# Attention 1 of a four-layer kernel: the sums over heads on GpSimd, two heads at a time, instead of strided sums on VectorE

## The chip, the cores and the metric

The kernel runs on one core of a Trainium2 chip. The time is device time in microseconds, the median of the timed runs. A core has five engines with a queue of their own each: TensorE (PE, with its weight loads shown as PEld), VectorE (DVE), ScalarE (ACT), GpSimd (POOL) and SyncE (SP), which here issues most DMAs. Engines wait for each other by semaphores that are written out by hand.

## The reference

Eight sequences of 256 tokens of width 256 go through four layers; each adds a cross attention over `ctx_1024` and then a feed-forward network. The change touches the attention of layer 1, whose softmax runs over the heads, not over the keys:

```python
    def _L1_xattn_ref(query, key, value, Wq_w, Wq_b, Wk_w, Wk_b, Wv_w, Wv_b, Wo_w, Wo_b):
        ...
        scale = 1.0 / jnp.sqrt(jnp.float32(HEAD_DIM))
        energy = jnp.einsum('bhqd,bhkd->bhqk', Qh, Kh) * scale
        attn = jax.nn.softmax(energy, axis=1)
        out = jnp.einsum('bhqk,bhkd->bhqd', attn, Vh)
        out = out.transpose(0, 2, 1, 3).reshape(b, -1, D_MODEL)
        return out @ Wo_w.T + Wo_b
```

With 16 heads of width 16, 256 queries and 256 keys, each (key, query) pair needs the maximum and the sum of 16 numbers, one for each head.

## The kernel before

The program goes through eight stages one after the other: attention 0, ffn 0, attention 1, ffn 1, and so on. Attention 1 lies from about 599 to 990 us of the profiled execution. It works in eight slots, one for each batch element `b`, and each slot handles two halves `t` of the keys (128 keys on the partitions; a row of `probs[:, t]` holds 16 heads x 256 queries in f32, 4096 elements).

In slot `b` (function `slot1` on each engine) the order is this:

- TensorE computes the scores once for the maxima (`for_maxima`, L871), two heads to a PSUM bank, first for `t` = 0, then for `t` = 1. Between them stand the products of the probabilities of the slot before with its values (`values1`, L808), which wait for the semaphore `norm1`.
- ScalarE copies the first two banks of each half to `M2` (L1361), VectorE takes the running maximum (L1802), folds it (L1804, L1806) and splits it in two bf16 parts (L1808, L1810).
- TensorE computes the scores a second time less the maxima (`less_maxima`, L885 and L888), ScalarE takes the exponentials two heads at a time (`exps1`, L1352, eight for each `t`, sixteen in a row), and each adds one to `exp1_done`.
- VectorE adds a bias to the values of the next element (`take_values`, L1722 and L1734) and then runs `sums1(b, 0)` and `sums1(b, 1)`. Each forms the sum over heads, its reciprocal (L1828) and the product of the 4096 probabilities with it (L1830, `norm1`). For `t` = 0 the sum is two reductions of eight heads (L1821) and an add (L1823), for `t` = 1 one reduction of sixteen (L1826); all read `probs` as "p h q -> p q h", so that neighbours in the reduction lie 256 elements apart. `rest_k` (L1697, `kr` <- `kf`, `KP`) stands between the two calls.
- After that VectorE still has `rest_q` (L1702), the residual (L1789), the statistics (L1606) and the low parts of keys and queries (L1706, L1710) before the maxima of the next slot.

GpSimd's part of attention 1 is one instruction ahead of the slots, `X` <- `X` + `bog` (L583, 128x4096 f32 with two inputs from SBUF). VectorE waits for it before slot 0. After it GpSimd has nothing until ffn 1. The routing stage of ffn 3 also has two adds of this kind on GpSimd (L630, 128x1280 bf16).

Of the kernel before, what the change touches and what calls it, by code (L numbers as in the profile page):

```python
# [12 lines left out]
ALU = mybir.AluOpType  # L13
ACT = mybir.ActivationFunctionType
AX = mybir.AxisListType
# [5 lines left out]
B, S = 8, 256  # L21
T = B * S
NT = T // P
ST = S // P
H, DH = 16, 16
HALF = 2
HPH = H // HALF
# [20 lines left out]
DIGIT_BITS, DIGITS, UNROLL0 = 2, 15, 3  # L48
# [25 lines left out]
def program(nc, a, out, stages):  # L74
    ctx = ExitStack()
    with ctx:
        def sem(name):
            return ctx.enter_context(nc.semaphore(name))

        def sb(name, shape, dt, c=ctx):  # L80
            return c.enter_context(nc.sbuf_tensor(name, shape, dt))
# [71 lines left out]
        probs = sb("probs", [P, ST, H, S], F32, att)  # L153
# [3 lines left out]
        hpart = sb("hpart", [P, 2, S], F32, att)  # L157
        hsum = sb("hsum", [P, ST, S], F32, att)
# [126 lines left out]
                 "xnt_psum xnt_done w_loaded qk_loaded bias_ready bias_added ctx0 ctx1 q_psum k_psum v_psum q_evac k_evac q_r1 "  # L285
                 "k_r1 q_mid k_mid q_split k_split pack0 pack1 pack_k0 pack_k1 padrow0 padrow1 v_copied v_ready smax_ps smax_done mT_ps m_hi m_lo mrow0 "
                 "mrow1 st_ps exp_done av_done o_out oT_ps on_rden on_norm o2_ps on_ready y_ps x_res mask_loaded mask_ready pad_out "
                 "nmax_ready rsum_ready vs_ready p1_ps p1_max m1_step m1_ready p2_ps exp1_done sum1_step norm1 av1_done x_ffn stored "
                 "pack_const pack_rows rt_const rt_logits rt_step rt_exp rt_cnt rt_prefix thr_step thr_cmp thr_cnt "
                 "xn_out0 xn_out1 xn_out2 xn_out3 rows_ready "  # L290
                 "experts_w0 experts_w1 experts_w2 experts_w3 experts_w4 experts_w5 experts_w6 experts_w7 "
# [4 lines left out]
                 "f3_router f3_place f3_gates f3_loaded f3_hot f3_list f3_idx "  # L296
                 "gather0 gather1 gather2 gather3 f3_xt f3_xgT f3_up f3_w1_act f3_w1_dve f3_mid f3_down f3_yg f3_scatter").split()
        s = {n: sem(n) for n in names}
        ctx_sem = [s["ctx0"], s["ctx1"]]
        pack = [s["pack0"], s["pack1"]]  # L300
        pack_k = [s["pack_k0"], s["pack_k1"]]
# [20 lines left out]
        def pack_keys(eng, par, done):  # L322
            for j, part in enumerate(K_PARTS):
                eng.dma_start(Kpack[par][DH * j:DH * (j + 1)].rearrange("d (e f) t -> d e (f t)", f=HALF),  # L324
                              KP[par][:, part]).then_inc(done, 16)
# [13 lines left out]
        def ready_x(eng, n):  # L339

            if n == 0:
                for half in range(2):
                    eng.wait_ge(s[f"x_load{half}"], 16)
                return
            kind, L = stages[n - 1]
            if kind == "att":
                eng.wait_ge(s["x_res"], FREE + 8 * (order["att", L] + 1))
            else:
                eng.wait_ge(s["x_ffn"], 1 + sum(k != "att" for k, _ in stages[:n - 1]))
# [194 lines left out]
        def _(pool):  # L544
# [26 lines left out]
            def attention(n, L):  # L571
                i = order["att", L]
                if n > 0:
                    ready_x(pool, n)
                if L in SOFTMAX_KEYS:
                    pool.wait_ge(s["k_split"], 8 * i + 1)
                    pool.wait_ge(s["pack_rows"], 64 * (m_order[L] + 1))
                    pack_keys(pool, 0, pack_k[0])

                if L != 0:  # L580
                    pool.wait_ge(s["bias_ready"], 2 * i + 2)
                    pool.wait_ge(s["xn_ready"], 8 * (ln_order["att", L] + 1))
                    pool.tensor_tensor(X[:], X[:], bog[:].unsqueeze(1).to_broadcast([P, NT, D]), ALU.add)\  # L583
                        .then_inc(s["bias_added"], 1)
                if L in SOFTMAX_KEYS:

                    for b in range(1, B):


                        pool.wait_ge(s["m_lo"], 8 * m_order[L] + b)  # L590
                        pack_keys(pool, b % 2, pack_k[b % 2])

            def rows_sent(n):

                pool.wait_ge(s["rows_ready"], 6 * 16 * (g_order[stages[n]] + 1))
                for j in range(LNB):
                    pool.wait_ge(xn_out[j], SENT0 + 16 * (PAIRS // LNB) * (g_order[stages[n]] + 1))
# [48 lines left out]
            for n, (kind, L) in enumerate(stages):  # L646
                if kind == "att":
                    attention(n, L)
                elif L in (0, 3):
                    (ffn0 if L == 0 else ffn3)(n)  # L650
                elif L == 1:
                    pool.wait_ge(s["f1_rmax"], 1)
                    pool.partition_all_reduce(rall[:], rmax[:], P, bass.bass_isa.ReduceOp.max).then_inc(s["f1_rall"], 1)
# [903 lines left out]
        def _(dve):  # L1557
# [105 lines left out]
            def attention(n, L):  # L1663
# [147 lines left out]

                def sums1(b, t):

                    steps = 4 if t == 0 else 2
                    base = 6 * b + 4 * t
                    if t == 0:

                        for half in range(2):
                            hh = slice(half * HPH, (half + 1) * HPH)
                            dve.wait_ge(s["exp1_done"], 16 * b + 4 * (half + 1))  # L1820
                            dve.tensor_reduce(hpart[:, half], probs[:, t, hh].rearrange("p h q -> p q h"), AX.X, ALU.add).then_inc(s["sum1_step"], 1)  # L1821
                        dve.wait_ge(s["sum1_step"], base + 2)
                        dve.tensor_tensor(hsum[:, t], hpart[:, 0], hpart[:, 1], ALU.add).then_inc(s["sum1_step"], 1)  # L1823
                    else:
                        dve.wait_ge(s["exp1_done"], 16 * (b + 1))
                        dve.tensor_reduce(hsum[:, t], probs[:, t].rearrange("p h q -> p q h"), AX.X, ALU.add).then_inc(s["sum1_step"], 1)  # L1826
                    dve.wait_ge(s["sum1_step"], base + steps - 1)
                    dve.reciprocal(hsum[:, t], hsum[:, t]).then_inc(s["sum1_step"], 1)  # L1828
                    dve.wait_ge(s["sum1_step"], base + steps)
                    dve.tensor_tensor(probs[:, t], probs[:, t], hsum[:, t].unsqueeze(1).to_broadcast([P, H, S]), ALU.mult)\  # L1830
                        .then_inc(s["norm1"], 1)

# [39 lines left out]
                def slot1(b, par, v):  # L1872
                    nearer, later = exists(b + 1), exists(b + 2)
                    maxima1(b, 0)
                    maxima1(b, 1)
                    if nearer:
                        take_values(b + 1, 1 - par)
                    sums1(b, 0)
                    if later:
                        rest_k(b + 2, par)  # L1880
                    sums1(b, 1)
                    if later:
                        rest_q(b + 2, par)
                    if exists(b - 1):
                        residual(b - 1)
                    if later:
                        low_k(b + 2, par)
                        low_q(b + 2, par)
# [285 lines left out]
            def route3(n):  # L2174
# [25 lines left out]
                for j in range(2):  # L2200
                    e = dve.tensor_tensor(row_m[:, j], row_m[:, 3 + j], row_m[:, 5], ALU.mult)
                chain(e)
                running_counts(2 * E3, lambda _, e: chain(e), 0, r)
                for j in range(PAIRS3):
                    of = slice(j * E3, (j + 1) * E3)
# [173 lines left out]
```

## Time and profile before

| | us |
|---|---|
| median of 3 runs | 2509.2 |
| lowest | 2507.66 |
| highest | 3518.86 |
| span of the profiled execution | 2506.0 |

Two of the three runs lie within 1.6 us of each other, the third stands alone. The profiled execution's span is 3.2 us below the median; those lie around the span. Engine busy times in the span: PE 2005.9 us, DVE 1279.5, ACT 810.5, POOL 242.8. Busy share is an average over eight stages with different limits. Attention 1 has its own: in the 401 us from 599 to 1000, DVE is busy for 356.28 us, PE for 261.48, ACT for 135.01 and POOL for 10.00, with a mean granted clock of TensorE of 0.80.

### The profile page before, as it was taken

To read this page: it belongs to the slowest core of one execution; us is meant where nothing else is said; L and a number is where in the kernel's file an instruction comes from. 1 tells how busy PE (TensorE), PEld (TensorE's weight loads), DVE (VectorE), ACT (ScalarE), POOL (GpSimd) and SP (SyncE) were. 2 spreads that over 40 slices of the span, in tenths; PEclk is the share of its full clock that TensorE was granted. 3 is DMA by queue.
4 is the path that set the end of the run, shared out by engine and by line. 5 is a ranking of instruction groups with operands and counts; after the bars stand their busy time and mean duration, and the time that the engine had idled before them with its cause. 6 is when DMAs were issued, how large, how long until landed. Compare 5 with 4: busy or idle time off the path is not lost.

```text
span 2506.0 us, 33028 instructions
## 1 busy us (share of the span) xinstructions
PE 2005.9 (80%) x11527; PEld 1280.2 (51%) x11528; DVE 1279.5 (51%) x2283; ACT 810.5 (32%) x1752; POOL 242.8 (10%) x234
## 2 busy tenths in 40 slices
PE   5999983594767755478998999999996676399998
PEld 3556543473534533334444444444444444389997
DVE  5334325516998997844442545453536666522221
ACT  3343331122433422334443521111115765122221
POOL 1010100341000000020110000000001000023333
PEclk9999995796878877579999999999998987599999
DMA  4342305126224210144431400000005541642222
GB/s 109 46 57 32 52 8 215 26 36 130 33 30 54 30 26 5 40 52 59 60 40 13 186 1 1 1 1 1 1 1 93 80 63 26 239 131 38 35 36 30
DMA packets 91386, 132.86 MB, mean 53 GB/s; under 512 B 13428, under 2 KB 80508, under 8 KB 88060
## 3 DMA queue, kind: packets, MB, share of 16 engines
q1 hardware_dynamic: 75900, 103.84, 19.7%
q0 software_dynamic: 15360, 27.28, 6.9%
q8 instruction: 86, 1.41, 0.3%
q14 instruction: 40, 0.33, 0.0%
HBM read 64.09 MB, written 16.26 MB: 32 GB/s over the span
## 4 chain that ended last, share of the span: by engine, by line
PE 59%; DVE 19%; DMA 8%; issue 6%; ACT 4%; SPq 4%; DVEq 0%; POOL 0%; POOLq 0%; ACTq 0%
PE ps L1137 13%; PE ps L808 10%; PE ps L1215 6%; PE ps L1226 5%; DMA Qpack<-QP 3%; PE ps L852 3%; PE ps L771 3%; PE ps L799 2%; DVE hpart L1821 2%; DVE hsum L1826 2%; DMA Kpack<-pad_rows 2%; SPq L446 2%; PE ps L1047 2%; PE ps L1037 2%; PE ps L1111 2%
## 5 line engine op out<-in xcount | busy, mean ns | idle before, releaser
L808 PE MATMUL ps<-pT,V 128*32 128x256 f32 x1536 | 298.5, 408 | 40.3 <-DVE V L1759 40.3
L1740 DVE TENSOR_REDUCE mx<-ps 128x2 f32<-128x512 f32 x256 | 165.6, 686 | 169.4 <-PE ps L774 92.5
L1337 ACT ACTIVATE pT<-ps 128x512 f32<-128x512 f32 x256 | 150.5, 597 | 243.2 <-PE ps L802 140.7
L799 PE MATMUL ps<-Qpack,Kpack 99*128 99x256 bf16 (+1 forms) x768 | 168.2, 289 | 40.5 <-ACT pT L1342 16.6
L808 PEld LDWEIGHTS ps<-pT,V 128*32 128x32 f32 x1536 | 104.7, 112 | 163.2 <-issue 63.3
L1215 PEld LDWEIGHTS ps<-xgT,XNT 128*128 128x128 f32 x1280 | 151.4, 194 | 2.0
L1215 PE MATMUL ps<-xgT,XNT 128*128 128x128 f32 x1280 | 151.5, 277 | 0.0
L1226 PE MATMUL ps<-w,mid 128*128 x640 | 144.6, 379 | 0.0
L771 PE MATMUL ps<-Kpack,Qpack 97*128 97x256 bf16 x512 | 107.9, 287 | 40.8 <-DMA Kpack<-pad_rows 22.7
L1342 ACT ACTIVATE pT<-ps,nmax 128x256 f32<-128x256 f32 x256 | 118.0, 496 | 56.5 <-DVE nmax L1750 55.7
L799 PEld LDWEIGHTS ps<-Qpack,Kpack 99*128 99x128 bf16 (+1 forms) x768 | 70.3, 102 | 123.1 <-ACT pT L1337 42.9
L808 PE MATMUL ps<-probs,V 128*32 128x256 f32 x512 | 66.5, 526 | 83.0 <-DVE probs L1830 83.0
L1226 PEld LDWEIGHTS ps<-w,mid 128*128 128x128 f32 x640 | 118.6, 190 | 14.5
L1137 PE MATMUL ps<-partA,h 128*128 128x512 bf16 x512 | 116.4, 379 | 0.2
L1137 PE MATMUL ps<-partB,h 128*128 128x512 bf16 x512 | 115.7, 379 | 0.0
L1750 DVE TENSOR_REDUCE nmax<-ps 128x2 f32<-128x512 f32 x128 | 84.6, 688 | 52.3 <-PE ps L799 51.8
L1533 ACT ACTIVATE mid<-ps 128x512 f32<-128x512 f32 x80 | 43.4, 595 | 208.2 <-PE ps L1215 202.9
L324 POOL DMA_DIRECT2D Kpack<-KP x96 | 51.2, 540 | 538.9 <-DVE MR L1745 453.7
L674 PE MATMUL ps<-ident,xn 128*128 128x128 f32 x224 | 43.8, 364 | 73.7 <-DVE xn L1656 64.5
L771 PEld LDWEIGHTS ps<-Kpack,Qpack 97*128 97x128 bf16 x512 | 44.8, 99 | 101.9 <-DVE mx L1740 41.3
L2113 DVE TENSOR_TENSOR xn<-hA 128x512 f32<-128x512 f32 x64 | 44.3, 692 | 102.8 <-ACT hA L1508 100.3
L583 POOL TENSOR_TENSOR X<-X,bog 128x4096 f32<-128x4096 f32 x3 | 26.4, 8814 | 627.2 <-DVE bog L1691 620.4
(312 smaller groups left out, 3733.0 us busy)
## 6 DMA issues: line engine op xcount, KB each, us to landing
Qpack<-QP SPq DMA_DIRECT2D x192, 128.0 KB, 6.9
w<-in_w SPq DMA_DIRECT2D x19, 1024.0 KB, 6.8
Kpack<-KP POOLq DMA_DIRECT2D x96, 128.0 KB, 5.6
Kpack<-KP SPq DMA_DIRECT2D x96, 128.0 KB, 4.2
ctxT<-in_ctxT SPq DMA_DIRECT2D x32, 256.0 KB, 5.9
h<-in_h SPq DMA_DIRECT2D x2, 4096.0 KB, 22.2
wd<-in_wd SPq DMA_DIRECT2D x4, 1536.0 KB, 14.9
xn_rows<-xn SPq DMA_DIRECT2D x16, 256.0 KB, 2.8
```

Source lines behind the costliest of these rows:

```text
L324: eng.dma_start(Kpack[par][DH * j:DH * (j + 1)].rearrange("d (e f) t -> d e (f t)", f=HALF), KP[par][:, part]).then_inc(done, 16)
L771: mm = pe.matmul(A[2 + h % 2][:, t], Qpack[par][0:MASK_ROW + 1, h, t * P:(t + 1) * P], Kpack[par][0:MASK_ROW + 1, h], start=True, stop=L != 0)
L799: mm = pe.matmul(A[h % ring][:, t], Kpack[par][0:rows, h, t * P:(t + 1) * P], Qpack[par][0:rows, h], start=True, stop=L != 0)
L808: mm = pe.matmul(O[c // 2][r0:r0 + VW, c % 2], V[par][:, t, h], weights[:, t], start=t == 0, stop=t == ST - 1)
L852: mm = pe.matmul(P1[:, t], lhs[:, c, t * P:(t + 1) * P], wo[:, c], start=c == 0, stop=c == tiles - 1)
L1137: mm = pe.matmul(bank, high(w_), part[:, v - 1, c] if v else high(src[:, c]), start=v + c == 0, stop=v == 2 and c == HT - 1)
L1215: mm = pe.matmul(bank[:, f % 4 * P:(f % 4 + 1) * P], w1_tile[k % 2][:, c, f * P:(f + 1) * P], xgT3[k % 2][:, c], start=c == 0, stop=c == K ...
L1226: mm = pe.matmul(ps[5 + 2 * (k % 2)][:, 0], mid3[k % 2][:, c], w2_3[:, ds(e, 1), c].squeeze(1), start=c == 0, stop=c == HT - 1)
L1337: act.activation(pT[h % 4][:], A[h % 2][:], ACT.Exp).then_inc(s["exp_done"], 1)
L1342: e = act.activation(pT[h % 8][:, t], A[h % 4][:, t], ACT.Exp, bias=nmax[:, t, h:h + 1], accum_out=esum[:, t, h:h + 1])
L1740: dve.tensor_reduce(mx[:, :, h], A[2 + h % 2][:], AX.X, ALU.max).then_inc(s["smax_done"], 1)
L1750: dve.tensor_reduce(nmax[:, :, h], A[h % 4][:], AX.X, ALU.max, negate=True).then_inc(s["nmax_ready"], 1)
```

## The change

In `sums1` on VectorE the three reductions and the add go. It now waits for `sum1_done`, then takes the reciprocal and multiplies as before. The new function `head_sums` on GpSimd makes the sum: for each `b` and `t` one add of two pairs of heads into `hpart` (128x512), six more adds of a pair each onto `hpart`, and one add of its two halves into `hsum[:, t]` (128x256). The seven adds wait for the exponentials pair by pair, and each waits for the add before it by `sum1_part`, a new name for the semaphore `thr_cnt`, which ffn 0 has left at 15 (`DIGITS`). The first add of a call waits for the end of the call before, the last add for `norm1` of the same half of the slot before. All sixteen calls follow on GpSimd's queue behind the add of L583.

```diff
...
-                 ... exp1_done sum1_step norm1 av1_done x_ffn stored "
+                 ... exp1_done sum1_done sum1_step norm1 av1_done x_ffn stored "
...
+        s["sum1_part"] = s["thr_cnt"]
...
@@ -582,6 +584,10 @@
                     pool.wait_ge(s["xn_ready"], 8 * (ln_order["att", L] + 1))
                     pool.tensor_tensor(X[:], X[:], bog[:].unsqueeze(1).to_broadcast([P, NT, D]), ALU.add)\
                         .then_inc(s["bias_added"], 1)
+                if L == 1:
+                    for b in range(B):
+                        for t in range(ST):
+                            head_sums(b, t)
                 if L in SOFTMAX_KEYS:
 
                     for b in range(1, B):
@@ -589,6 +595,22 @@
 
                         pool.wait_ge(s["m_lo"], 8 * m_order[L] + b)
                         pack_keys(pool, b % 2, pack_k[b % 2])
+
+            def head_sums(b, t):
+
+                k = DIGITS + 7 * (ST * b + t)
+                pool.wait_ge(s["exp1_done"], 16 * b + 8 * t + 2)
+                if b + t:
+                    pool.wait_ge(s["sum1_done"], ST * b + t)
+                pool.tensor_tensor(hpart[:], probs[:, t, 0:2], probs[:, t, 2:4], ALU.add).then_inc(s["sum1_part"], 1)
+                for e in range(2, H // 2):
+                    pool.wait_ge(s["exp1_done"], 16 * b + 8 * t + e + 1)
+                    pool.wait_ge(s["sum1_part"], k + e - 1)
+                    pool.tensor_tensor(hpart[:], hpart[:], probs[:, t, 2 * e:2 * e + 2], ALU.add).then_inc(s["sum1_part"], 1)
+                pool.wait_ge(s["sum1_part"], k + 7)
+                if b:
+                    pool.wait_ge(s["norm1"], ST * (b - 1) + t + 1)
+                pool.tensor_tensor(hsum[:, t], hpart[:, 0], hpart[:, 1], ALU.add).then_inc(s["sum1_done"], 1)
 
             def rows_sent(n):
 
@@ -1811,22 +1833,9 @@
 
                 def sums1(b, t):
 
-                    steps = 4 if t == 0 else 2
-                    base = 6 * b + 4 * t
-                    if t == 0:
-
-                        for half in range(2):
-                            hh = slice(half * HPH, (half + 1) * HPH)
-                            dve.wait_ge(s["exp1_done"], 16 * b + 4 * (half + 1))
-                            dve.tensor_reduce(hpart[:, half], probs[:, t, hh].rearrange("p h q -> p q h"), AX.X, ALU.add).then_inc(s["sum1_step"], 1)
-                        dve.wait_ge(s["sum1_step"], base + 2)
-                        dve.tensor_tensor(hsum[:, t], hpart[:, 0], hpart[:, 1], ALU.add).then_inc(s["sum1_step"], 1)
-                    else:
-                        dve.wait_ge(s["exp1_done"], 16 * (b + 1))
-                        dve.tensor_reduce(hsum[:, t], probs[:, t].rearrange("p h q -> p q h"), AX.X, ALU.add).then_inc(s["sum1_step"], 1)
-                    dve.wait_ge(s["sum1_step"], base + steps - 1)
+                    dve.wait_ge(s["sum1_done"], 2 * b + t + 1)
                     dve.reciprocal(hsum[:, t], hsum[:, t]).then_inc(s["sum1_step"], 1)
-                    dve.wait_ge(s["sum1_step"], base + steps)
+                    dve.wait_ge(s["sum1_step"], 2 * b + t + 1)
                     dve.tensor_tensor(probs[:, t], probs[:, t], hsum[:, t].unsqueeze(1).to_broadcast([P, H, S]), ALU.mult)\
                         .then_inc(s["norm1"], 1)
```

## Rows read from the trace of the kernel before

**Rows 1.** The page: span, and busy time of each engine.
```profile
span 2506.0 us, 33028 instructions
PE 2005.9 (80%) x11527; PEld 1280.2 (51%) x11528; DVE 1279.5 (51%) x2283; ACT 810.5 (32%) x1752; POOL 242.8 (10%) x234
```

**Rows 2.** Waits, 599 to 1000 us: waiter <- releaser: total us, times, longest.
```profile
PE ps L808 <- DVE probs L1830: 83.0, 8, 16.5
```

**Rows 3.** Chain that ended last, 765 to 815 us: start us, us, what.
```profile
769.01 7.34 DVE hpart L1821 x2
...
783.64 7.03 DVE hsum L1826
```

**Rows 4.** Timeline of DVE, 757 to 860 us: start us, us, engine, line, operation.
```profile
768.05 0.49 DVE L1734 COPY V<-Vb 128x256 f32<-128x256 f32 x2
769.01 7.33 DVE L1821 TENSOR_REDUCE hpart<-probs 128x256 f32<-128x2048 f32 x2 [0.46 <-ACT probs L1352]
776.37 0.43 DVE L1823 TENSOR_TENSOR hsum<-hpart 128x256 f32<-128x256 f32 x1
776.83 1.75 DVE L1828 RECIPROCAL hsum<-hsum 128x256 f32<-128x256 f32 x1
778.61 4.42 DVE L1830 TENSOR_TENSOR probs<-probs,hsum 128x4096 f32<-128x4096 f32 x1
782.96 0.68 DVE L1697 TENSOR_TENSOR kr<-kf,KP 128x512 f32<-128x512 f32 x1
783.56 7.10 DVE L1826 TENSOR_REDUCE hsum<-probs 128x256 f32<-128x4096 f32 x1
790.70 1.75 DVE L1828 RECIPROCAL hsum<-hsum 128x256 f32<-128x256 f32 x1
792.48 4.43 DVE L1830 TENSOR_TENSOR probs<-probs,hsum 128x4096 f32<-128x4096 f32 x1
```

**Rows 5.** ACT: one line's instructions (durations ns min/median/max), then its timeline.
```profile
L1352 ACT ACTIVATE probs<-ps x128: 597/597/599, 625.6 to 964.2; 128x512 f32<-128x512 f32 x128
...
766.38 10.60 ACT L1352 ACTIVATE probs<-ps 128x512 f32<-128x512 f32 x16 [2.70 <-PE ps L888]
...
814.07 10.55 ACT L1352 ACTIVATE probs<-ps 128x512 f32<-128x512 f32 x16 [2.70 <-PE ps L888]
```

**Rows 6.** POOL: one line's instructions, then its timeline in the first microseconds.
```profile
L583 POOL TENSOR_TENSOR X<-X,bog x3: 8799/8822/8822, 599.1 to 1902.6; 128x4096 f32<-128x4096 f32 x3
...
1.50 0.29 POOL L547 TENSOR_SCALAR_AFFINE_SELECT ident<-ident 128x128 f32<-128x128 f32 x1 [0.49 <-POOL ident L545]
...
2.42 0.19 POOL L555 MEMSET ones_bf<- 128x128 bf16 x1
2.69 0.29 POOL L557 TENSOR_SCALAR_AFFINE_SELECT upto<-upto 128x128 bf16<-128x128 bf16 x1
...
4.51 0.19 POOL L569 TENSOR_SCALAR spare<-row 128x1 f32<-128x1 f32 x1
```

**Rows 7.** POOL and DVE at the same time: timelines, and durations of single lines.
```profile
1902.63 8.82 POOL L583 TENSOR_TENSOR X<-X,bog 128x4096 f32<-128x4096 f32 x1 [591.15 <-DVE bog L1691]
1904.62 7.37 DVE L1697 TENSOR_TENSOR kr<-kf,KP 128x512 f32<-128x512 f32 x1 [1.54 <-ACT KP L1305]
...
L1734 DVE COPY V<-Vb x16: 278/290/8479, 599.5 to 911.5; 128x256 f32<-128x256 f32 x16
...
L630 POOL TENSOR_TENSOR lists<-lists,part x2: 2327/2950/3572, 2182.3 to 2184.5; 128x1280 bf16<-128x1280 bf16 x2
...
2182.28 3.66 DVE L2233 TENSOR_TENSOR lists<-lists,col 128x1280 bf16<-128x1280 bf16 x1 [0.15 <-DVE lists L2230]
...
2188.39 1.48 DVE L2235 TENSOR_TENSOR lists<-lists,part 128x1280 bf16<-128x1280 bf16 x1
```

**Rows 8.** Windows: engines' busy us (x count), granted clock, DMA share, GB/s.
```profile
788.00:797.00 9.00, 0.81 (x7) 0.25 (x8) 8.93 (x4) 0.42 (x1) 0.00 (x0) 0.55 0.00 0
801.00:805.00 4.00, 4.00 (x26) 1.54 (x28) 3.22 (x6) 0.00 (x0) 0.00 (x0) 0.50 0.84 143
```

More of the change, by code:

```diff
@@ L287, in program @@
                  "mrow1 st_ps exp_done av_done o_out oT_ps on_rden on_norm o2_ps on_ready y_ps x_res mask_loaded mask_ready pad_out "
-                 "nmax_ready rsum_ready vs_ready p1_ps p1_max m1_step m1_ready p2_ps exp1_done sum1_step norm1 av1_done x_ffn stored "
+                 "nmax_ready rsum_ready vs_ready p1_ps p1_max m1_step m1_ready p2_ps exp1_done sum1_done sum1_step norm1 av1_done x_ffn stored "
                  "pack_const pack_rows rt_const rt_logits rt_step rt_exp rt_cnt rt_prefix thr_step thr_cmp thr_cnt "
```

## The prediction, made before the changed kernel ran

> **What bounds the kernel now.** The page's engine totals [rows 1] say little here, since they mix eight stages, so I read attention 1 alone. The waits of its stretch come first [rows 2]: TensorE waits eight times, once a slot, for `probs` of L1830, 83.0 us in all, up to 16.5 us at a time. TensorE is not the limit of the slot's second half. The chain that ended last [rows 3] then shows who is: from the fourth exponential on it stays on VectorE, through the two reductions of L1821 and, after `kr`, the one of L1826. The timeline of VectorE [rows 4] gives one slot in full: 7.33 us for the two reductions, 0.43 for the add, 1.75 for the reciprocal, 4.42 for the product, `kr`, 7.10 for the third reduction, 1.75, 4.43, with no gap to speak of. The second product ends at 792.48 + 4.43 = 796.9 us, and TensorE's value products and VectorE's remaining duties both start from there. The exponentials are much shorter: the burst of sixteen begins at 766.38, the next slot's at 814.07 [rows 5], a period of 47.7 us, of which 796.9 - 766.4 = 30.5 us pass from the first exponential to the end of the second product. All that the change touches lies in these 30.5 us. The other 17 us start at the end of the second product and move with it.
>
> **What it removes.** Per slot, 7.33 + 0.43 + 7.10 = 14.9 us of VectorE, all on the chain: 8 x 14.9 = 119 us, if nothing took their place.
>
> **What it adds: the price of an add on GpSimd.** The trace has no f32 add of 128x512 there. The nearest row is L583, the same kind of add with 4096 elements, 8.82 us at most [rows 6]. In proportion, 512 elements take 8.82 / 8 = 1.10 us, and that is the lower bound, since it leaves out what an instruction costs whatever its size. An instruction on a single element a partition (L569) takes 0.19 us. With that as the fixed part, each element costs (8820 - 190) / 4095 = 2.11 ns, so 512 elements cost 0.19 + 1.08 = 1.27 us and 256 cost 0.73 us. I take these. (The Trainium skill, GPSIMD Engine Reference, section 3.1, gives 4497 ns for such an add of 2048 elements; a line through that figure and L583 would give 1.28 us for 512, so the sum would stay.) Each add also waits for the one before. The gap between dependent GpSimd instructions is 2.69 - (2.42 + 0.19) = 0.08 us between L555 and L557, and 0.49 us between L545 and L547 [rows 6]. I take 0.08, since L547 is the first of its kind in the program and may pay for that; 0.49 stays as the upper bound. One call is then 7 x (1.27 + 0.08) + 0.73 + 0.08 = 10.3 us, and two calls 20.5 us. At 1.10 us, 0.55 us and the same gap it is 8.9 us a call, and at a gap of 0.49 us it is 7 x 1.76 + 1.22 = 13.5 us. So GpSimd adds up more slowly than VectorE did (10.3 against 7.8 or 7.1 us), and any gain must come from lying beside other work.
>
> **What of it lies beside other work.** The exponentials are spaced (10.60 - 0.60) / 15 = 0.67 us, and the second one ends at 766.38 + 0.67 + 0.60 = 767.65 [rows 5]. GpSimd starts there, 1.36 us before VectorE could at 769.01. After that the exponentials come twice as fast as the adds, so it never waits for one again. While it makes the second sum, VectorE has the first reciprocal, the first product and `kr`: 1.75 + 4.42 + 0.68, 6.8 us that used to stand in the chain in full. This is where the change could win.
>
> **What takes it back.** The rows of both engines at the same time [rows 7] show that a GpSimd add and some VectorE instructions exclude each other for their whole length. While L583 ran from 1902.63 to 1911.45, VectorE's `kr` (two f32 inputs in SBUF, 0.69 us otherwise) took 7.37 us and ended at 1911.99. A copy `V` <- `Vb`, 0.29 us as a rule, took 8.48 us under another L583. It works in both directions: of the two L630 adds the first took 2.33 us and held up L2233 (3.66 us against 1.48 for L2235, the same shape), and the second, queued while L2233 finished, took 3.57 us. The product of L1830 has both inputs, `probs` and `hsum`, in SBUF, as `kr` has. I therefore count its 4.42 us and those of `kr` one after the other with GpSimd's adds, not beside them. (By the Trainium skill, SBUF — State Buffer, section "Who interferes with whom", a VectorE instruction with two SBUF inputs contends with a GpSimd instruction that reads SBUF, the second fully blocked, while one with a single input outside the 2-port modes does not contend. The trace agrees for `kr` and L2233. On the reciprocal the rule would leave the sum as it stands, and no row here shows it.) I let the reciprocal, with one input, run beside an add.
>
> **The sum for one slot**, on the clock of [rows 4]. GpSimd starts at 767.7. The two copies of L1734 (0.49 us, a form that was excluded in [rows 7]) get between its first adds: 0.5 us. First call 10.3 us: the first sum is ready at 778.5, where it was ready at 776.8 before. The reciprocal runs to 780.3 beside the first adds of the second call. The product waits for the add in progress, then holds GpSimd off for 4.4 us, and `kr` may follow at once, 0.6 us. The second call thus takes 10.3 + 4.4 + 0.6 = 15.3 us and ends at 793.8. Then reciprocal 1.75, product 4.43 and 0.1 us between instructions: 800.0, against 796.9. Each slot gets about 3 us longer. Which engine wins the port first hardly matters, because both sums, one product and `kr` must go through it in a row before the second reciprocal can start.
>
> Eight slots x 3.0 us = 24 us. The last slot has no `kr`, which changes it by 0.6. The profiled execution would take 2506.0 + 24 = 2530 us. The median of the runs shown lies 3.2 us above it, so 2533 us. TensorE's longer idle time costs nothing besides: its granted clock falls to the lower level of 1.2 GHz in this wait already (0.55 on the mean, 788 to 797 us) and is still there, at 0.50, from 801 to 805 us [rows 8], and those cold products are in the 17 us.
>
> The other pieces cost nothing. GpSimd's queue is empty in attention 1 but for L583, which ends before slot 0, and the change moves no DMA. The wait on `norm1` of the slot before has long been met. Behind VectorE's wait for the first sum stand `kr` and, from there on, the parts and residual of later elements. `kr` moves from 783.0 to 785.7 at the earliest, and its successors feed a slot that begins 28 us later. VectorE's idle 9 us or so while it waits gain nothing, since its order is fixed. If the cover of the first product is gone altogether, that is the sum above already.
>
> **Rivals.**
> 1. *No exclusion for L1830.* If the product runs beside the adds, the second sum is ready at 767.7 + 20.5 = 788.2 to 788.7, and the product ends 6.3 us later, at 794.5 to 795: 2 to 2.4 us a slot won, 16 to 19 us in all, about 2492. With adds of 1.10 us it is about 2470. For it: L1830 reads `hsum` as a broadcast, which no excluded row does. Against it: three instructions of [rows 7] were held up, with bf16 and f32 operands. It decides only if the product is exempt.
> 2. *Dearer adds.* The path has sixteen GpSimd instructions a slot, so each 0.1 us more on one of them costs 1.6 us a slot or 13 us in all. At the gap of 0.49 us each slot is 3.0 + 2 x 3.2 = 9.5 us longer, 2585 us. At 0.2 us more on each the change passes 2% (50 us). For it: two waits stand before each add where L557 had one. Against it: the gap between L555 and L557.
> 3. *Cheaper adds with exclusion*, 1.10 us: 3.0 - 2 x 1.4 = 0.2 us a slot, 2511 us. That is the break-even point of the forecast, and only an instruction with no fixed cost reaches it.
> 4. *The reciprocal excluded too.* Then up to 1.75 us a slot more, 2547 us.
>
> **How the numbers follow.** Exclusion and adds between the bounds, with cases 3 and 4 as its edges, 2505 to 2559 us: 0.73, best guess 2533. Dearer adds, beyond 2559 us: 0.15. No exclusion, below 2505 us: 0.12, of which 0.02 reaches 2459 us or less. The measurement can tell about 2% from no change, 50 us here, 2459 and 2559 us. So faster 0.02, same 0.83, slower 0.15. Range 2500 to 2563 us: below it lies most of the no-exclusion case (0.09), above it the rest of the dearer adds (0.11).
>
> **What would show each step.** Adds on GpSimd with a shortest duration of 1.27 us for 128x512 and 0.73 for 128x256; a pitch of 1.35 us in a row of them. In each slot one product of L1830 longer than 4.43 us, by what was left of the add in progress, and one GpSimd add of some 5 us that was held up behind it. `sum1_done` of the first half 12 us after the first exponential, the second product's end 33.6 us after it, a period of 50.7 us. VectorE idle some 9 us in the middle of a slot and again some 7 us after `kr`. A product of 4.42 us with GpSimd busy all through it would refute the exclusion; a pitch above 1.55 us would make the time pass 2%.

## The result, and the profile of the changed kernel

| | before | changed |
|---|---|---|
| median | 2508.43 us (4 runs) | 2527.7 us (4 runs) |
| lowest to highest, but for one run | 2503.28 to 2509.2 | 2524.25 to 2532.53 |
| span of the profiled execution | 2506.0 | 2526.3 |

The ratio is 1.0088 (95% interval 1.007 to 1.0106): 0.9% slower, inside 2%. The forecast was 2533 us, in a range of 2500 to 2563. The one run left out, of 3518.86 us, stands alone; what lengthened it is not known.

VectorE is less busy and GpSimd more, as the change means it. The page, first the span, then each engine's busy us and instructions; compare [rows 1] of the kernel before:

```profile
span 2526.3 us, 33213 instructions
PE 2005.2 (79%) x11489; PEld 1281.5 (51%) x11528; DVE 1185.0 (47%) x2251; ACT 812.3 (32%) x1752; POOL 429.7 (17%) x362
```

VectorE lost 94.5 us of busy time, GpSimd gained 186.9, and the span grew by 20.3. The waits of attention 1, 599 to 1020 us, say why nothing was won (waiter <- releaser: total us, times, longest; [rows 2] before):

```profile
DVE hsum L1837 <- POOL hsum L613: 126.1, 16, 10.9
PE ps L830 <- DVE probs L1839: 96.9, 8, 17.8
```

VectorE now stands still for 126.1 us until GpSimd's sums come, and TensorE's wait for the product grew from 83.0 to 96.9 us. One slot as ScalarE, VectorE and GpSimd saw it (timelines: start us, us, engine, line, operation), to be laid beside [rows 4] and [rows 5]:

```profile
775.49 10.55 ACT L1374 ACTIVATE probs<-ps 128x512 f32<-128x512 f32 x16 [2.70 <-PE ps L910]
...
777.18 1.27 DVE L1756 COPY V<-Vb 128x256 f32<-128x256 f32 x2
787.46 1.75 DVE L1837 RECIPROCAL hsum<-hsum 128x256 f32<-128x256 f32 x1 [9.01 <-POOL hsum L613]
789.25 5.27 DVE L1839 TENSOR_TENSOR probs<-probs,hsum 128x4096 f32<-128x4096 f32 x1
794.45 1.75 DVE L1719 TENSOR_TENSOR kr<-kf,KP 128x512 f32<-128x512 f32 x1
802.36 1.75 DVE L1837 RECIPROCAL hsum<-hsum 128x256 f32<-128x256 f32 x1 [6.17 <-POOL hsum L613]
804.15 4.42 DVE L1839 TENSOR_TENSOR probs<-probs,hsum 128x4096 f32<-128x4096 f32 x1
...
776.83 1.27 POOL L605 TENSOR_TENSOR hpart<-probs 128x512 f32<-128x512 f32 x1 [25.25 <-ACT probs L1374]
778.24 8.39 POOL L609 TENSOR_TENSOR hpart<-hpart,probs 128x512 f32<-128x512 f32 x6
786.71 0.72 POOL L613 TENSOR_TENSOR hsum<-hpart 128x256 f32<-128x256 f32 x1
787.57 1.26 POOL L605 TENSOR_TENSOR hpart<-probs 128x512 f32<-128x512 f32 x1
788.98 12.55 POOL L609 TENSOR_TENSOR hpart<-hpart,probs 128x512 f32<-128x512 f32 x6
801.61 0.72 POOL L613 TENSOR_TENSOR hsum<-hpart 128x256 f32<-128x256 f32 x1
```

Read it on a clock that starts with the slot's first exponential. GpSimd starts after 1.3 us. Its first sum releases VectorE after 12.0 us, where the old sum did after 10.5 us (776.83 - 766.38). The six adds of L609 take 8.39 us in the first call and 12.55 us in the second, beside the product. From the first reciprocal to the second it is 14.90 us, 13.87 before. The second product ends after 33.1 us, 30.5 before. So 1.5 us of each slot's loss come from the late first sum and 1.0 us from the stretch behind it: 2.5 us x 8 = 20 us, the 20.3 us of the span. The whole stage agrees: from its first exponential to the end of its last product it took 358.5 us before and takes 379.2 now, 20.7 us more.

The held-up instruction shows in the line's own durations (ns min/median/max, first and last start us):

```profile
L609 POOL TENSOR_TENSOR hpart<-hpart,probs x96: 1259/1267/5261, 628.7 to 996.8; 128x512 f32<-128x512 f32 x96
L605 POOL TENSOR_TENSOR hpart<-probs x16: 1261/1266/1268, 627.3 to 984.4; 128x512 f32<-128x512 f32 x16
L613 POOL TENSOR_TENSOR hsum<-hpart x16: 721/722/729, 637.1 to 998.2; 128x256 f32<-128x256 f32 x16
L1839 DVE TENSOR_TENSOR probs<-probs,hsum x16: 4424/4848/5284, 639.7 to 1000.7; 128x4096 f32<-128x4096 f32 x16
```

An add takes 1.27 us, yet some take 5.26, 4.0 us longer, which is nearly a whole product. 96 adds of 1.27 us would be 122 us and the line was busy for 155.4, so there are some eight such adds, one in each slot.

### The profile page after: what moved, and what is told of

Read it like the earlier page. It is cut to its first block, busy times and chain, and to the rows that moved or that the text cites. A ratio compares the mean times of both kernels' runs of the same rounds, so it can differ in the third digit from the quotient of the medians.

```text
span 2526.3 us, 33213 instructions
## 1 busy us (share of the span) xinstructions
PE 2005.2 (79%) x11489; PEld 1281.5 (51%) x11528; DVE 1185.0 (47%) x2251; ACT 812.3 (32%) x1752; POOL 429.7 (17%) x362
## 3 DMA queue, kind: packets, MB, share of 16 engines
q8 instruction: 86, 1.41, 0.3%
## 4 chain that ended last, share of the span: by engine, by line
PE 58%; DVE 13%; POOL 7%; DMA 7%; issue 6%; ACT 4%; SPq 4%; DVEq 0%; POOLq 0%; ACTq 0%
PE ps L1159 13%; PE ps L830 10%; POOL hpart L609 6%; PE ps L1237 6%; PE ps L1248 5%; DMA Qpack<-QP 3%; PE ps L874 3%; PE ps L793 3%; PE ps L821 2%; DMA Kpack<-pad_rows 2%; SPq L448 2%; PE ps L1069 2%; PE ps L1059 2%; ACT pT L1364 2%; PE ps L1133 2%
## 5 line engine op out<-in xcount | busy, mean ns | idle before, releaser
L609 POOL TENSOR_TENSOR hpart<-hpart,probs 128x512 f32<-128x512 f32 x96 | 155.4, 1619 | 13.8
L830 PE MATMUL ps<-probs,V 128*32 128x256 f32 x512 | 67.2, 534 | 96.9 <-DVE probs L1839 96.9
## 6 DMA issues: line engine op xcount, KB each, us to landing
wd<-in_wd SPq DMA_DIRECT2D x4, 1536.0 KB, 14.8
```

The costliest lines, as they stand in the source:

```text
L609: pool.tensor_tensor(hpart[:], hpart[:], probs[:, t, 2 * e:2 * e + 2], ALU.add).then_inc(s["sum1_part"], 1)
L830: mm = pe.matmul(O[c // 2][r0:r0 + VW, c % 2], V[par][:, t, h], weights[:, t], start=t == 0, stop=t == ST - 1)
```

## The experiments

Theory 1 is that of the prediction: a GpSimd add costs 1.27 us with its gap on top, the adds lie on the path, and the product of L1830 and the adds exclude each other, so that nearly none of the product is hidden. The rivals were that the exclusion plays no part, and that the adds' number or form is what costs.

### The product left out, a reduction with one input in its place

In the changed kernel:

```diff
-                    dve.tensor_tensor(probs[:, t], probs[:, t], hsum[:, t].unsqueeze(1).to_broadcast([P, H, S]), ALU.mult)\
+                    dve.tensor_reduce(stand[:, t], probs[:, t].rearrange("p h (q e) -> p (h q) e", e=16), AX.X, ALU.add)\
                         .then_inc(s["norm1"], 1)
```

> The changed kernel with the product of the probabilities by the reciprocal left out; in its place VectorE runs a reduction over the same 4096 elements, which has one SBUF input (the output is that of unnormalised probabilities). In the changed kernel each slot lasts 33.1 us from the first exponential to the end of the second product, and the second call of adds lasts 14.8 us there, 4.2 us more than the first. Theory 1, product and adds exclude each other: with one input the reduction runs beside the adds, the second call shrinks to 10.6 us (11.3 if kr still gets between), the slot by 3.5 to 4.2 us, the kernel from about 2528 to 2494 to 2500 us, after taking off what the second run shows for the stand-in's own length. Rival, the adds are simply slow and the second call is long for another reason (waits for exponentials, its own queue): 14.8 us again and 2528 us.

And the same edit in the kernel before, which gives the price of the stand-in:

> The kernel before with the same stand-in reduction in place of the product; the output is that of unnormalised probabilities. GpSimd is idle beside it, so it gives only the length of the stand-in d against 4.42 us: the time should move by 16 x (d - 4.42) us, near zero if a reduction of 4096 adjacent elements takes about 4.3 to 4.4 us, so 2505 to 2510 us. Theory 1 and its rival expect the same here.

Measured: 2497.16 us (2494.05 to 2498.87) for the first, ratio to the kernel before 0.9962 (0.9948 to 0.9976), and 2506.41 us for the second, ratio 0.9999 (0.9989 to 1.0009). The stand-in has the product's length within 5 ns (4420 against 4425), and by itself moves nothing. Beside it GpSimd's second call runs nearly as fast as its first; timelines of VectorE and GpSimd in the first of these kernels, then the two lines' durations:

```profile
775.02 1.75 DVE L1838 RECIPROCAL hsum<-hsum 128x256 f32<-128x256 f32 x1 [9.02 <-POOL hsum L614]
776.81 4.42 DVE L1840 TENSOR_REDUCE stand<-probs 128x256 f32<-128x4096 f32 x1
785.96 1.75 DVE L1838 RECIPROCAL hsum<-hsum 128x256 f32<-128x256 f32 x1 [3.36 <-POOL hsum L614]
...
776.54 8.59 POOL L610 TENSOR_TENSOR hpart<-hpart,probs 128x512 f32<-128x512 f32 x6
...
L610 POOL TENSOR_TENSOR hpart<-hpart,probs x96: 1260/1268/1528, 628.6 to 965.2; 128x512 f32<-128x512 f32 x96
L1840 DVE TENSOR_REDUCE stand<-probs x16: 4419/4420/4421, 639.6 to 969.1; 128x256 f32<-128x4096 f32 x16
```

The six adds take 8.59 us instead of 12.55, no add takes longer than 1.53 us, and the reduction reads `probs` beside them without losing time. From reciprocal to reciprocal it is 10.94 us instead of 14.90. So 4.0 us a slot, 30.5 us between the medians, are the exclusion's, and a reduction with one input over the same data is free of it. Without it the change would have gained 0.4%, not lost, which is rival 1, the one that ends on the other side: its time of about 2492 us compares with 2497.16 here. That the second call was slow for a reason of its own is refuted.

The stand-in differs from the product in more than its inputs: it writes 256 elements, not 4096, and to another tile. Two rows of the changed kernel bear on that. `kr` shares no tile with the adds, writes only 512 elements and was held up all the same (1.75 us instead of 0.68). `Vb` also writes 512 elements and has two inputs, but one of them, `ps`, lies in PSUM; it overlapped an add by 0.3 us and neither got longer (VectorE's, then GpSimd's timeline):

```profile
825.90 0.69 DVE L1744 TENSOR_TENSOR Vb<-ps,bv 128x512 f32<-128x512 f32 x1
...
826.28 1.27 POOL L605 TENSOR_TENSOR hpart<-probs 128x512 f32<-128x512 f32 x1 [23.95 <-ACT probs L1374]
```

So neither the shared tile nor the size of the output is needed. Two inputs in SBUF are not the whole of it either: the copies of L1756 have one and were held up, two of them taking 1.27 us here instead of 0.49.

### One half of the keys on GpSimd, the other as before

First the sum of the first half (`t` = 0) alone on GpSimd; on VectorE:

```diff
...
+                    if t == 0:
+                        dve.wait_ge(s["sum1_done"], b + 1)
+                    else:
+                        dve.wait_ge(s["exp1_done"], 16 * (b + 1))
+                        dve.tensor_reduce(hsum[:, t], probs[:, t].rearrange("p h q -> p q h"), AX.X, ALU.add).then_inc(s["sum1_step"], 1)
...
```

> Only the sum of the first half of the keys on GpSimd, the second half as before by one strided reduction on VectorE. No add runs beside a product. Theory 1: the first sum is ready 11.9 us after the first exponential, against 10.4 us before, and all after it is as before, so 1.5 us a slot and 12 us in all more than before: about 2520 us. Rival, the whole loss comes from the exclusion and none from the late first sum: about 2508 us.

Measured: 2519.86 us (2518.23 to 2521.87), ratio 1.0057 (1.004 to 1.0074), 13 us more than the kernel before. ScalarE's and VectorE's timelines of one slot:

```profile
769.61 10.55 ACT L1373 ACTIVATE probs<-ps 128x512 f32<-128x512 f32 x16 [2.70 <-PE ps L909]
...
781.58 1.75 DVE L1842 RECIPROCAL hsum<-hsum 128x256 f32<-128x256 f32 x1 [9.00 <-POOL hsum L612]
```

The first sum releases the reciprocal 781.58 - 769.61 = 12.0 us after the first exponential, and both products take 4.42 us, undisturbed. The rival that put all of the loss on the exclusion falls: over half of it is the late first sum.

The other way round, the sum of the second half on GpSimd in a tile `hpool`, the first half by strided reductions:

```diff
-                pool.wait_ge(s["exp1_done"], 16 * b + 8 * t + 2)
+                pool.wait_ge(s["exp1_done"], 16 * b + 10)
...
-                pool.tensor_tensor(hpart[:], probs[:, t, 0:2], probs[:, t, 2:4], ALU.add).then_inc(s["sum1_part"], 1)
+                pool.tensor_tensor(hpool[:], probs[:, 1, 0:2], probs[:, 1, 2:4], ALU.add).then_inc(s["sum1_part"], 1)
```

> Only the sum of the second half on GpSimd (in a tile of its own), the first half as before by strided reductions on VectorE. GpSimd can start with the tenth exponential, 6.7 us after the first. Theory 1, exclusion: its call takes 10.6 + 4.4 + 0.4 + 0.6 = 16 us and ends 22.8 us after the first exponential, reciprocal and product end at 29.0 against 30.5 us before: 1.5 us a slot gained, about 2496 us. Rival, no exclusion: the call ends at 17.3 us, the slot at 23.6 us: 6.9 us a slot gained, about 2453 us. A second rival, that GpSimd's sums lose whatever lies beside them: 2508 us or more.

Measured: 2482.2 us (2480.62 to 2485.17), ratio 0.9909 (0.9892 to 0.9926), 25 us less than before where 12 were expected. Timelines of ScalarE, VectorE and GpSimd in one slot:

```profile
756.77 10.60 ACT L1374 ACTIVATE probs<-ps 128x512 f32<-128x512 f32 x16 [2.70 <-PE ps L910]
...
759.40 7.38 DVE L1842 TENSOR_REDUCE hpart<-probs 128x256 f32<-128x2048 f32 x2 [0.46 <-ACT probs L1374]
766.81 1.02 DVE L1844 TENSOR_TENSOR hsum<-hpart 128x256 f32<-128x256 f32 x1
...
769.66 4.99 DVE L1850 TENSOR_TENSOR probs<-probs,hsum 128x4096 f32<-128x4096 f32 x1
774.58 1.75 DVE L1719 TENSOR_TENSOR kr<-kf,KP 128x512 f32<-128x512 f32 x1
...
778.29 1.75 DVE L1848 RECIPROCAL hsum<-hsum 128x256 f32<-128x256 f32 x1 [1.96 <-POOL hsum L613]
780.08 4.42 DVE L1850 TENSOR_TENSOR probs<-probs,hsum 128x4096 f32<-128x4096 f32 x1
...
763.45 1.28 POOL L605 TENSOR_TENSOR hpool<-probs 128x512 f32<-128x512 f32 x1 [29.47 <-ACT probs L1374]
764.87 12.58 POOL L609 TENSOR_TENSOR hpool<-hpool,probs 128x512 f32<-128x512 f32 x6
777.53 0.72 POOL L613 TENSOR_TENSOR hsum<-hpool 128x256 f32<-128x256 f32 x1
```

The direction and the mechanism are those expected, the size was missed by half: the call was held up once, by the product, and ended 21.5 us after the first exponential; no exclusion would have given 17.3 us. Its length was 14.8 us and not 16. I had added the short add of L1844 and `kr` to GpSimd's time in full. It is VectorE that waited for them instead: the add took 1.02 us where it takes 0.43 alone, and GpSimd lost next to nothing. The second product ended 27.7 us after the first exponential, 2.8 us sooner than before, and 8 x 2.8 = 22 us lies within the interval of the measured gain (19 to 27 us). The strided reductions, with one input, ran 7.38 us beside the adds (7.33 before).

This also answers whether GpSimd's sums lose wherever they stand: they don't. With an early start beside work that doesn't exclude them, half of them gain.

### The same pairs on VectorE

```diff
-                        for half in range(2):
...
-                            dve.tensor_reduce(hpart[:, half], probs[:, t, hh].rearrange("p h q -> p q h"), AX.X, ALU.add).then_inc(s["sum1_step"], 1)
...
+                    dve.tensor_tensor(hpart[:], probs[:, t, 0:2], probs[:, t, 2:4], ALU.add).then_inc(s["sum1_step"], 1)
+                    for e in range(2, H // 2):
+                        dve.wait_ge(s["exp1_done"], at + e + 1)
+                        dve.wait_ge(s["sum1_step"], k + e - 1)
+                        dve.tensor_tensor(hpart[:], hpart[:], probs[:, t, 2 * e:2 * e + 2], ALU.add).then_inc(s["sum1_step"], 1)
```

> The same sums over pairs of heads behind the exponentials as in the change, in the same order and number, but on VectorE. An add of 128x512 from SBUF takes 0.69 us there (L1804 before), with its gap 0.73. Theory 1, the engine is what costs and not the way of summing: first sum ready 7.7 us after the first exponential (10.4 before), second sum in 5.55 us instead of 7.1, so 4.2 us a slot gained, 34 us in all: about 2474 us. Rival, sixteen short instructions with a wait each lose against three long reductions: 2508 us or more.

Measured: 2472.61 us (2467.87 to 2473.24), ratio 0.9858 (0.9841 to 0.9874). The sums are those of the change, instruction for instruction, on the other engine: 55 us less than the changed kernel. ScalarE's and VectorE's timelines:

```profile
753.12 10.55 ACT L1352 ACTIVATE probs<-ps 128x512 f32<-128x512 f32 x16 [2.70 <-PE ps L888]
...
755.21 0.69 DVE L1817 TENSOR_TENSOR hpart<-probs 128x512 f32<-128x512 f32 x1
755.93 4.33 DVE L1821 TENSOR_TENSOR hpart<-hpart,probs 128x512 f32<-128x512 f32 x6
760.29 0.42 DVE L1823 TENSOR_TENSOR hsum<-hpart 128x256 f32<-128x256 f32 x1
760.75 1.75 DVE L1825 RECIPROCAL hsum<-hsum 128x256 f32<-128x256 f32 x1
...
774.80 4.42 DVE L1827 TENSOR_TENSOR probs<-probs,hsum 128x4096 f32<-128x4096 f32 x1
```

A sum over 16 heads takes 5.5 us in this form, 7.1 to 7.8 us as a strided reduction, and 10.6 us on GpSimd. The way of summing was a gain; the engine took it away.

### Four heads in an add on GpSimd

```diff
+                pool.tensor_tensor(hfour[:], probs[:, t, 0:4], probs[:, t, 4:8], ALU.add).then_inc(s["sum1_part"], 1)
+                for e in range(2, H // 4):
...
+                    pool.tensor_tensor(hfour[:], hfour[:], probs[:, t, 4 * e:4 * e + 4], ALU.add).then_inc(s["sum1_part"], 1)
+                pool.wait_ge(s["sum1_part"], k + 3)
+                pool.tensor_tensor(hfour[:, 0:2], hfour[:, 0:2], hfour[:, 2:4], ALU.add).then_inc(s["sum1_part"], 1)
```

> The change with four heads in an add on GpSimd: three adds of 1024 elements, one of 512, one of 256 in place of seven of 512 and one of 256, the same number of additions in all. If an instruction costs 0.19 us plus 2.11 ns an element plus a gap of 0.14 us, a 1024 add takes 2.35 us and a call 9.7 us instead of 10.6, but the first can start only with the fourth exponential, 1.3 us later: the first sum comes 0.4 us later, the second call is 0.9 us shorter, 0.4 us a slot gained, about 2525 us against 2528. Rival, the cost lies in the number of instructions (waits of 0.3 us and more each): 2515 us or less.

Measured: 2521.82 us (2517.51 to 2529.09), ratio to the kernel before 1.0054 (1.0038 to 1.0071), against 1.0088 (1.007 to 1.0106) for the change. The intervals touch, so the time alone doesn't settle whether it is better than the change, and the span of the profiled execution, 2527.0 us, was no shorter. The trace of attention 1 tells more (durations of a single line, as above, then ScalarE's and VectorE's timelines):

```profile
L609 POOL TENSOR_TENSOR hfour<-hfour,probs x32: 2339/2353/6342, 631.3 to 989.0; 128x1024 f32<-128x1024 f32 x32
...
772.91 10.55 ACT L1376 ACTIVATE probs<-ps 128x512 f32<-128x512 f32 x16 [2.70 <-PE ps L912]
...
791.75 2.83 DVE L1721 TENSOR_TENSOR kr<-kf,KP 128x512 f32<-128x512 f32 x1
...
800.75 4.43 DVE L1841 TENSOR_TENSOR probs<-probs,hsum 128x4096 f32<-128x4096 f32 x1
```

The second product ends 800.75 + 4.43 - 772.91 = 32.3 us after the first exponential, 0.8 us sooner than in the change where 0.4 were expected, and the stage took 373.6 us against 379.2. These 5.6 us are close to the 5.9 between the medians. The rest of that execution, which the edit doesn't touch, took 6.3 us longer, and so the span hides them.

2.35 us for 1024 elements, 1.27 for 512 and 0.72 for 256 lie on one line: 2.12 ns an element and 0.18 us fixed. Larger adds save the fixed part, and VectorE waits longer for the one in progress: `kr` took 2.83 us, 1.75 in the changed kernel and 0.68 before. The gap between two dependent adds is 0.14 us, as in the change. Waits of 0.3 us and more for each instruction, the rival, are refuted.

### The second half as a tree over adjacent heads, on VectorE

```diff
+                        dve.tensor_tensor(htree[:], probs[:, t, 0:8], probs[:, t, 8:16], ALU.add).then_inc(s["sum1_step"], 1)
+                        for w in (4, 2):
+                            k += 1
+                            dve.wait_ge(s["sum1_step"], k)
+                            dve.tensor_tensor(htree[:, 0:w], htree[:, 0:w], htree[:, w:2 * w], ALU.add).then_inc(s["sum1_step"], 1)
```

> Sums on VectorE: the first half in pairs behind the exponentials, the second half as a tree over adjacent halves of the heads (adds of 2048, 1024, 512 and 256 elements, about 4.5 us). Theory 1 and the price of 1.07 ns an element of a VectorE add with two SBUF inputs: 1.0 us a slot less than the version with pairs in both halves, about 2466 us. Rival, wide adds of that kind are slower an element than 1.07 ns, as the strided reductions are (1.73 ns): the tree takes 7 us and the time is 2486 us or more.

Measured: 2468.85 us (2462.3 to 2471.76), ratio 0.984 (0.9822 to 0.9858). ScalarE's and VectorE's timelines:

```profile
750.13 10.55 ACT L1352 ACTIVATE probs<-ps 128x512 f32<-128x512 f32 x16 [2.70 <-PE ps L888]
...
764.49 2.28 DVE L1826 TENSOR_TENSOR htree<-probs 128x2048 f32<-128x2048 f32 x1
766.81 1.95 DVE L1830 TENSOR_TENSOR htree<-htree 128x1024 f32<-128x1024 f32 x2
768.79 0.43 DVE L1833 TENSOR_TENSOR hsum<-htree 128x256 f32<-128x256 f32 x1
...
771.04 4.43 DVE L1837 TENSOR_TENSOR probs<-probs,hsum 128x4096 f32<-128x4096 f32 x1
```

The wide add takes 2.28 us for 2048 elements, 1.1 ns each, so the rival of slow wide adds is refuted. The tree takes 4.7 us, 0.8 us less than the pairs. The second product ends 25.3 us after the first exponential (771.04 + 4.43 - 750.13), 26.1 with the pairs, and the stage took 318.4 us against 326.2. Whether the whole time is shorter stays open: the medians differ by 4 us, the two intervals overlap, and in the profiled executions, one of each kernel, the rest of the program took back 6.3 of the 7.8 us. The tree has the lowest median of all kernels here, 38 us under the kernel before and 59 us under the change.

## Why the prediction was right, point by point

- **What bounds the slot.** Right. VectorE's sums and products set it, and every kernel's time followed the end of the second product. It came 33.1 us after the first exponential for 2527.7 us, 32.3 for 2521.8, 32.0 for 2519.9, 30.5 for 2508.4, 29.1 for 2497.2, 27.7 for 2482.2, 26.1 for 2472.6 and 25.3 for 2468.9 us. Eight slots make about 8 us of time for each 1 us of slot.
- **The price of an add.** 1.27 and 0.73 us forecast, 1.27 and 0.72 measured. The gap between dependent adds was sized at 0.08 us and measured 0.14 (778.24 - 776.83 - 1.27), so a call took 10.6 us, not 10.3. The gap of 0.49 us, on which rival 2 rested, did not come back. One slip stands beside it: the line that the prediction drew through L583 and the 4497 ns for 2048 elements of the Trainium skill, GPSIMD Engine Reference, section 3.1, gives an estimate of 1.25 us for 512, not 1.28; the sum didn't use it.
- **The exclusion.** Right, and shown by the stand-in. It was the deciding step, since without it the sign turns. It was sized at the product's 4.4 us and held GpSimd up by 4.0 (5.26 - 1.27). The one argument for rival 1, that no excluded row reads a broadcast, was mistaken: L2233, held up in [rows 7], reads `col` as a broadcast. The rows of before spoke more clearly for the exclusion than the forecast said.
- **Short instructions in between.** Mis-sized. The copies of L1756 (0.5 us) and `kr` (0.6 us) were charged to GpSimd. GpSimd lost next to nothing to the copies: its second add started 1.41 us after the first, as undisturbed ones do, and VectorE's copies waited, 1.27 us where they took 0.49. `kr` cost it at most the 0.26 us by which the longest add in the stand-in kernel exceeds 1.27. So the forecast had 0.5 us too much for the copies, 0.4 for the product and 0.4 for `kr`, and 0.8 too little for the two calls' gaps. Together they make the slot of 33.6 us forecast and 33.1 measured, 8 x 0.5 = 4 us of the 5 by which the forecast was high. That it came so close is in part luck: these errors offset each other. (`kr` is missing from the last two slots, not from the last alone; both are 0.3 us shorter than the others.)
- **The reciprocal.** It ran 1.75 us beside the adds, as assumed, and no add was held up by it: rival 4 is out. The Trainium skill, SBUF — State Buffer, section "Who interferes with whom", says that VectorE instructions with one SBUF input outside the 2-port modes don't contend and those with two do against GpSimd reads. By that rule the stand-in, the strided reductions and the reciprocal had to run free and the products not, and the traces agree in all four: 4.42, 7.38, 1.75 us undisturbed, and 5.27 for the product.
- **The rest of the slot and TensorE's clock.** Taken as 17 us that move with the second product, at no charge for the clock. In the sum that is right: the mean granted clock of the stage was 0.80 before and 0.79 after, and the mean of the seven periods grew from 46.96 to 49.50 us, as much as the slot's first part. In a single slot it isn't. Before, this rest lasted 17.1 to 17.3 us in the four middle slots, at a granted clock of 0.74 in each; in the changed kernel it lasted 17.7 us at 0.71 in the third slot and 16.4 us at 0.78 in the fourth, which is the one shown. The period of that one grew by 1.8 us only, to 49.4 and not to the 50.7 forecast. What makes the granted clock differ from slot to slot no run here tests.

## What to carry to other kernels

Before work goes from VectorE to GpSimd, list what VectorE will do at that time and look for the same forms beside GpSimd in a trace. Here the instructions with two inputs in SBUF stood in line with GpSimd's adds and hid nothing, the copies with one input had to wait too, and only reductions, reciprocals and an add with one input in PSUM ran beside them. A dependent chain pays its own length, so the receiving engine must either be as fast or start that much sooner; here the half that could start during other reductions gained 25 us and the whole lost 19. And separate the form from the engine: the pairs over adjacent heads were worth 34 us where the reductions had stood.

## What the runs showed of the hardware that I had not expected

- A short VectorE instruction with two inputs pays by waiting for the GpSimd add in progress (`kr` 1.75 and 2.83 us instead of 0.68, behind adds of 1.27 and 2.35 us), but costs GpSimd hardly anything (longest add 1.53 us). Part of it falls in the 0.14 us gap; where the rest goes no run here shows. Only the long product held an add up by 4.0 us.
- The price of a GpSimd add follows one line from 256 to 1024 elements, 0.18 us + 2.12 ns an element, and reaches L583's 8.82 us for 4096 within 0.05 us.
- A reduction on VectorE whose neighbours lie 256 elements apart costs 7.10 us for 4096 elements, one over adjacent elements 4.42 us.
